# Merge rows of a batched eigensolver: the scan over gap parts, live flags from a count, rank in four passes

## What is computed

```python
def _L2_gnn_ref(features, A, W0, b0, W1, b1):
    deg = jnp.sum(A, axis=-1)
    d_isqrt = jax.lax.rsqrt(deg)
    Lap = deg[..., :, None] * jnp.eye(n, dtype=A.dtype) - A
    Lap_norm = d_isqrt[..., :, None] * Lap * d_isqrt[..., None, :]
    _, U = jnp.linalg.eigh(Lap_norm)
    agg = jnp.einsum('bmn,bmd->bnd', U, features)
    h = jax.nn.relu(jnp.einsum('bnd,hd->bnh', agg, W0) + b0)
    out = jnp.einsum('bnh,oh->bno', h, W1) + b1
    return jnp.einsum('bnm,bmo->bno', U, out)
x = _layernorm(x + _L0_gnn_ref(...)); x = _layernorm(x + _L1_gnn_ref(...))
x = _layernorm(x + _L2_gnn_ref(x, adj, ...)); x = _layernorm(x + _L3_gnn_ref(...))
```

## Time and profile before

| | us |
|---|---|
| three runs of the kernel | 6776.52, 6777.59, 6789.82 |
| median | 6777.59 |
| the profiled execution, whole time | 6779.89 |
| the profiled execution, span | 6778.1 |

### The profile page before, as it was taken

One profiled execution on the slowest core, in us unless ns is written; L12 is line 12 of the kernel. 1 busy time (PEld: TensorE's weight loads), 2 busy tenths in 40 slices (PEclk: granted clock), 3 DMA queues, 4 the chain that ended last, 5 costly groups with the idle time before them and its releaser, 6 DMA issues.

```text
span 6778.1 us, 60058 instructions
## 1 busy us (share of the span) xinstructions
PE 2516.6 (37%) x16082; PEld 1645.2 (24%) x16082; DVE 5267.2 (78%) x19535; ACT 1080.2 (16%) x3167; POOL 1128.3 (17%) x1482
## 2 busy tenths in 40 slices
PE   1444444443292726447251171000682000100476
PEld 0121222222141414233141161000571000100354
DVE  5666666666899999999669887999798999999300
ACT  0000000001223222231220030000230000000255
POOL 0000000000344444444412031000420000100000
PEclk9666666655586767758575585555795555555688
DMA  4000000000000000000120004000002000100110
GB/s 112 14 16 25 14 16 16 18 20 25 18 13 7 13 7 10 3 7 0 19 52 0 0 7 94 0 0 0 7 13 95 25 0 19 43 0 0 37 50 13
DMA packets 150157, 140.40 MB, mean 21 GB/s; under 512 B 36685, under 2 KB 136666, under 8 KB 142938
## 3 DMA queue, kind: packets, MB, share of 16 engines
q1 hardware_dynamic: 149850, 136.97, 7.4%
HBM read 110.43 MB, written 26.41 MB: 20 GB/s over the span
## 4 chain that ended last, share of the span: by engine, by line
DVE 70%; PE 17%; DMA 5%; issue 3%; ACT 3%; SPq 1%; POOL 1%; DVEq 0%; ACTq 0%; POOLq 0%; PEldq 0%
PE psum L1818 7%; DVE big_b L1033 3%; DVE big_a L1041 2%; DVE big_a L1043 2%; DVE ms L1044 2%; DVE ms L1077 2%; DVE big_b L1076 2%; DVE big_b L634 2%; DVE gvec L364 2%; DVE big_b L647 2%; DVE big_b L1037 2%; DVE big_b L1031 1%; PE psum L1838 1%; DVE big_b L637 1%; DMA big_b<-rows_dram 1%
## 5 line engine op out<-in xcount | busy, mean ns | idle before, releaser
L1818 PE MATMUL psum<-big_a 128*32 128x508 f32 (+59 forms) x4032 | 444.6, 612 | 39.6 <-ACT big_a L1781 39.6
L1961 PE MATMUL psum<-plane,big_b 128*128 128x128 f32 x192 | 36.8, 371 | 934.3 <-DVEq L1157 917.9
L1276 DVE RECIPROCAL f_ln<-f_ln 128x16 f32<-128x16 f32 x20 | 5.1, 253 | 432.4 <-ACT f_ln L1385 430.9
L1951 PE MATMUL psum<-big_b 128*128 128x128 f32 x384 | 70.5, 369 | 652.2 <-ACT big_b L1899 652.2
L1641 POOL TENSOR_TENSOR big_a<-big_a,plane 128x2048 f32<-128x2048 f32 x28 | 183.5, 6554 | 759.8 <-ACT big_a L1605 625.9
L1471 PE MATMUL psum<-plane,big_a 128*128 128x128 f32 x192 | 50.1, 429 | 674.3 <-ACT big_a L1392 652.7
L1868 ACT ACTIVATE ms<-ms 128x64 f32<-128x64 f32 (+1 forms) x36 | 8.7, 243 | 1800.6 <-DVE ms L1097 1648.8
L701 POOL TENSOR_TENSOR big_b<-big_b 128x128 f32<-128x128 f32 x615 | 286.0, 465 | 48.3
L696 POOL TENSOR_TENSOR big_b<-big_b 128x512 f32<-128x512 f32 (+1 forms) x164 | 168.3, 1026 | 739.9 <-DVEq L526 730.3
L1982 POOL MEMSET big_b<- 128x2304 f32 x1 | 2.0, 2022 | 1646.8 <-DVEq L415 1646.8
L700 POOL TENSOR_TENSOR big_b<-big_b 128x128 f32<-128x128 f32 x615 | 260.3, 423 | 48.2
(11 more groups left out here) (669 smaller groups left out, 10604.4 us busy)
## 6 DMA issues: line engine op xcount, KB each, us to landing
big_a<-rows_dram SPq DMA_DIRECT2D x4, 4096.0 KB, 12.2
vt<-pairs_dram SPq DMA_DIRECT2D x504, 32.0 KB
big_a<-rows_dram SPq DMA_DIRECT2D x4, 2048.0 KB, 17.0
big_a<-rows_dram SPq DMA_DIRECT2D x2, 3072.0 KB, 15.0
big_b<-rows_dram SPq DMA_DIRECT2D x2, 3072.0 KB, 22.0
big_b<-adj SPq DMA_DIRECT2D x2, 2048.0 KB, 17.5
big_b<-adjT SPq DMA_DIRECT2D x2, 2048.0 KB, 39.2
lap_dram<-big_b SPq DMA_DIRECT2D x4, 1024.0 KB, 11.2
```

Source lines behind the costliest of these rows:

```text
L1818: ins = t.matmul(psum[i * SPAN:i * SPAN + MW, 0, 0:4 * wide], v_masked[:, i, q * MW:(q + 1) * MW], anode[:, g:g + 4, k + 1:N + 2 * u], sta ...
L1951: ins = t.matmul(bank(4, g), deflate[:, g, :], w_full[:, g, :], start=True, stop=True)
```

## The change

**Rank.** The first pass now forms the difference of the pair. Two later passes are replaced by passes that compare the difference with zero and combine in one instruction. There are four passes in front of the reduction where there were five.

**Live flags.** Live entries sort ahead of the others (dead ones have the key 100), so the sorted flags are `slot < number of live entries`. `live_j`, its copies and its turn in the sort loop go; a reduction over the flags (`n_live`) and one comparison on 64x128 (new L818) come.

**Scan.** The state carried from step to step is no longer the gathered weight and place. It is three values: the products `x` and `w` of the gap with the shares of the two weights, and the sum `t` of the two weights. These are formed for all neighbours ahead of the scan on whole rows (new L860 to L868), as if nothing merged. At each step the test is `x*w < tol`, written three times over as a mask; beside it the values for the case that the pair does merge are formed in `sc_t`. A predicated copy then puts them over the three values of the next pair where the mask is set. After the scan, four instructions on whole rows make the gathered weights and places (new L905 to L908). `sc_t` and `scan_h` get more rows.

```diff
-            d_j, z_j, rank_j, key_j, live_j = (side(width) for _ in range(5))
+            d_j, z_j, rank_j, key_j = (side(width) for _ in range(4))
...
-                st.go(v.tensor_copy(live_j[part], live[:, cols_j]))
...
-            st.go(v.tensor_tensor(pair, inner(key_j), outer(d_i), ALU.is_equal))
+            st.go(v.tensor_tensor(pair, inner(key_j), outer(d_i), ALU.subtract))
             st(v.tensor_tensor(pair2, jota, outer(slot_i), ALU.is_lt))
-            st(v.tensor_tensor(pair, pair, pair2, ALU.mult))
-            st(v.tensor_tensor(pair2, inner(key_j), outer(d_i), ALU.is_lt))
-            st(v.tensor_tensor(pair, pair, pair2, ALU.add))
+            st(v.scalar_tensor_tensor(pair2, pair, 0.0, pair2, ALU.is_equal, ALU.mult))
+            st(v.scalar_tensor_tensor(pair, pair, 0.0, pair2, ALU.is_lt, ALU.add))
...
-            for src, dst in ((d_j, g_ds), (z_j, g_zs), (live_j, g_on)):
+            n_live = gs[:, 26:26 + nb]
+            st.go(v.tensor_reduce(n_live, blocks(live), X, ALU.add))
+            for src, dst in ((d_j, g_ds), (z_j, g_zs)):
...
+            st(v.tensor_tensor(blocks(g_on[:, :]), over(pl["iota"][0:B, 0:blk], nb, 1), over(n_live, blk, 2), ALU.is_lt))
...
+            st.go(v.tensor_tensor(later(at_d), later(at_p), earlier(at_p), ALU.subtract))
+            st.go(v.tensor_copy(earlier(at_next), later(at_z)))
+            st(v.tensor_tensor(later(at_t), later(at_z), earlier(at_z), ALU.add))
+            st(v.reciprocal(later(at_r), later(at_t)))
+            st.go(v.tensor_tensor(later(at_x), earlier(at_z), later(at_r), ALU.mult))
+            n_w = st.go(v.tensor_tensor(later(at_w), later(at_z), later(at_r), ALU.mult))
+            st.after(n_w)
+            st.go(v.tensor_tensor(later(at_x), later(at_x), later(at_d), ALU.mult))
+            st(v.tensor_tensor(later(at_w), later(at_w), later(at_d), ALU.mult))
...
             for k in range(1, blk):
-                n_t = lp.go(v.tensor_tensor(t_, q0, zk, ALU.add))
-                n_d = lp.go(v.tensor_tensor(dd_, at(r_far), bf(r_far), ALU.subtract))
-                if nb < 4:
-                    lp.after(n_t)
-                    n_h = lp.go(v.scalar_tensor_tensor(h_, t_, r_tol2, t_, ALU.mult, ALU.mult))
-                    n_i = lp.go(v.reciprocal(rt, t_))
-                    lp.after(n_d)
-                    n_r = lp.go(v.scalar_tensor_tensor(r_, q0, zk, dd_, ALU.mult, ALU.mult))
-                    lp.after(n_i)
-                    n_x = lp.go(v.scalar_tensor_tensor(x_, q0, rt, dd_, ALU.mult, ALU.mult))
-                    lp.after(n_r)
-                    lp(v.scalar_tensor_tensor(at(r_close), r_, dd_, h_, ALU.mult, ALU.is_lt))
-                    lp.go(v.scalar_tensor_tensor(at(r_q), q0, at(r_close), zk, ALU.mult, ALU.add))
-                    lp(v.scalar_tensor_tensor(at(r_far), x_, at(r_close), at(r_far), ALU.mult, ALU.subtract, reverse1=True))
+                if more:
+                    n_t = lp.go(v.tensor_tensor(tmp(2), at(at_t), at(at_next), ALU.add))
+                if nb < 4:
+                    n_c = lp.go(v.scalar_tensor_tensor(at(at_c, 3), many(at(at_x), 3), at(at_w), tol_many, ALU.mult, ALU.is_lt))
...
+                if more:
+                    lp.go(v.tensor_tensor(dd_, fields(at_d)[..., k + 1], at(at_x), ALU.add))
+                    lp.after(n_t)
+                    n_r = lp.go(v.reciprocal(r_, tmp(2)))
...
+                        lp.after(n_r)
+                        n_x = lp.go(v.scalar_tensor_tensor(tmp(0, 2), at(at_t, 2), r_, many(dd_, 2), ALU.mult, ALU.mult))
+                    lp.after(n_x)
+                    lp(v.copy_predicated(fields(at_s, 3)[..., k + 1], at(at_c, 3).bitcast(U32), merged))
...
+            st.go(v.tensor_copy(fields(at_q), fields(at_z)))
+            st(v.tensor_tensor(later(at_r), later(at_c), later(at_x), ALU.mult))
+            st.go(v.copy_predicated(later(at_q), later(at_c).bitcast(U32), later(at_t)))
+            st(v.tensor_tensor(later(at_p), later(at_p), later(at_r), ALU.subtract))
```

More of the change, by code:

```diff
@@ L201, in graph_net @@
         g_onout = sb("g_onout", [B, N])
-        sc_t = sb("sc_t", [128, 7, NL // 2])
+        sc_t = sb("sc_t", [128, 8, NL // 2])
         rank_c = sb("rank_c", [N, GB])
@@ L723, in graph_net @@
         sc_w = big_a[0:B, 0:17 * N].rearrange("g (i n) -> g i n", n=N)
-        scan_h = big_a[:, 17 * N:17 * N + 6 * 64].rearrange("p (i n) -> p i n", n=64)
+        scan_h = big_a[:, 17 * N:17 * N + 12 * 64].rearrange("p (i n) -> p i n", n=64)
         ms = sb("ms", [N, 30, B])
@@ L841, in v_level_rows @@
             tall = slice(0, nb * B) if wide else slice(0, B)
[L842 to L845, removed]
+            cols_t = 4 if nb == 4 else 1
+            if wide:
+                at_p, at_q, at_z, at_c, at_s, at_d, at_r = 0, 1, 2, 3, 6, 10, 11
+                fields = lambda i, n=1: scan_h[tall, i:i + n, 0:blk]
+                r_tol2 = gs_h[tall, 38:39]
+                for b in range(nb):
+                    half = slice(b * B, (b + 1) * B)
+                    st.go(v.tensor_copy(scan_h[half, at_p, 0:blk], pd[:, b, :]))
+                    st.go(v.tensor_copy(scan_h[half, at_z, 0:blk], zk2[:, b, :]))
+                    st(v.tensor_copy(gs_h[half, 38:39], tol2[:, b:b + 1]))
+            else:
+                at_p, at_q, at_z, at_c, at_s, at_d, at_r = 0, 1, 5, 2, 10, 14, 15
+                fields = lambda i, n=1: sc_w[:, i:i + n, :].rearrange("g f (b i) -> g f b i", b=nb) if nb == 4 else sc_w[:, i:i + n, :]
+                r_tol2 = tol2
@@ new lines, in v_level_rows @@
+            later = lambda i, n=1: fields(i, n)[..., 1:]
+            earlier = lambda i, n=1: fields(i, n)[..., :blk - 1]
+            at_x, at_w, at_t, at_next = range(at_s, at_s + 4)
+            st.go(v.tensor_tensor(later(at_d), later(at_p), earlier(at_p), ALU.subtract))
[3 more added lines that the diff above has]
+            st.go(v.tensor_tensor(later(at_x), earlier(at_z), later(at_r), ALU.mult))
@@ new lines, in v_level_rows @@
+            n_w = st.go(v.tensor_tensor(later(at_w), later(at_z), later(at_r), ALU.mult))
+            st.after(n_w)
+            st.go(v.tensor_tensor(later(at_x), later(at_x), later(at_d), ALU.mult))
+            st(v.tensor_tensor(later(at_w), later(at_w), later(at_d), ALU.mult))
+            tmp = lambda i, n=1: sc_t[tall, i:i + n, 0:cols_t] if nb == 4 else sc_t[tall, i:i + n, 0]
+            merged, dd_, r_, y_, part_ = tmp(0, 3), tmp(3), tmp(4), tmp(5), tmp(6, 2)
+            many = lambda ap, n: ap.broadcast_to([ap.shape[0], n] + list(ap.shape[2:]))
@@ L895, in v_level_rows @@
-            if wide:
-                for b in range(nb):
-                    half = slice(b * B, (b + 1) * B)
-                    for dst, src in ((pd, r_far), (pq, r_q)):
-                        st.go(v.tensor_copy(dst[:, b, :], src[half, 0, :]))
-                    st(v.tensor_copy(close[:, b, :], r_close[half, 0, :]))
+                    for dst, src in ((pd, at_p), (pq, at_q)):
+                        st.go(v.tensor_copy(dst[:, b, :], scan_h[half, src, 0:blk]))
+                    st(v.tensor_copy(close[:, b, :], scan_h[half, at_c, 0:blk]))
+            else:
+                st(v.tensor_copy(close, sc(at_c)))
```

51 lines of the change are left out of this document (20 added, 31 removed).

## The result

The changed kernel takes 6712.22 us (median of 4 runs, 6705.95 to 6719.83), the kernel before 6779.45 beside it. The ratio is 0.9899, 95% interval 0.9881 to 0.9916. The prediction was 6706, with 6694 to 6726 as its range. The profiled execution took 6709.86 us, its span is 6708.1, 70.0 shorter than before.

A forecast was written before the change was run, and what follows sets the result against it. DVE bounds lev 1 and 2 only until ACT's turns do (29.25, 40.75 us); at lev 0 DVE already waits. Savings 2 + 29.3 + 41 = 72.3 us off 6779.89, less 2.3 to the median, gave 6706, range 6694 to 6726.

The follow-up runs named there:

- e6: Changed kernel with ACT's root moved into each level's last turn and, there, SP storing the rows before the turn: 6674.64 us, ratio 0.9855 to the kernel before.

## What to carry to other kernels

Before you sum up what a shorter engine program saves, find its hand-overs to other engines and read how long the partner has been idle at each: that idle time, and no more, is what the saving is worth there. When it is used up, the next microseconds come from the order of work on the partner, and such a move is worth nothing before the engine is early enough. Check a result by the lengths of the stages that were changed, since a whole time can come out as forecast for a reason that has nothing to do with the edit.

## What the runs showed of the hardware

- A predicated copy of three elements a partition takes 0.16 to 0.17 us, that of 64 elements 0.22; three-wide and one-wide combined instructions both take 0.21. In a chain of instructions as small as these the number of instructions counts, not whether each writes one element or three.
- The rows of lev 0, with the same DVE instructions up to the pass in question, took 142.1 or 139.7 us, by whether a POOL instruction came just after or just before the start of that pass: the stall of 4.2 us puts the later meetings of the two engines elsewhere. A saving of 2 us in such a place isn't a property of the edit.
- A store of 224 KB took 3.0 us to land 13 us behind one of 1024 KB, 5.8 right behind it, and 4.3 when it was issued 8 us ahead of it, in e6. Loads that waited for the larger store started 5.1 us behind it, and those that waited for a small store right behind it started 6.3 behind it: when both must have landed, the order is worth 1 us here.
